# A recurrence that normalises its own input and output: two layer-norm stages folded into the LSTM loop of a hybrid convolution, attention and expert network

## The chip, the cores and the metric

The kernel runs on one core of a Trainium2 chip. A core has five engines that work side by side: PE (TensorE, matrix products), DVE (VectorE), ACT (ScalarE), POOL (GpSimd) and SP (SyncE, which here issues the DMAs). They wait for one another only through semaphores and through the barrier between two stages. The metric is the device time of one execution in microseconds (us). Before the change the median of three runs is 1300.95 us (1299.09 to 1301.1).

## The reference, cut to what matters

The network has many layers; this change touches the part between the slice attention and the sigmoid attention. The activations are 32 images of 64 channels by 256 positions, held on chip in `xa` as 128 partitions (two halves of the batch times 64 channels) by 4096 columns (16 images by 256 positions).

```
h = layernorm(x)                     # over the 64 channels, eps 1e-5        "ln3"
for t in range(256):                 # LSTM over the 256 positions, 32 sequences
    g = tanh(h_t U_c + s V_c + b_c);  i, o = sigmoid(h_t U_i + s V_i + b_i), sigmoid(... o ...)
    c = f * c + i * g                # the kernel keeps the cell in a scaled form
    s = o * tanh(c);  y_t = s
x = x + y                            # the residual
h = layernorm(x)                     # "ln4", the input of the sigmoid attention
```

A layer norm here is three steps: take the mean over 64 channels away (a product with the matrix `center`), sum the squares over the channels, and multiply with one over the root of the variance plus 1e-5.

## The kernel before, in words

The program is a row of stages. Each stage opens a block in which every engine has its own instruction list, and ends with a barrier of all engines; the next stage starts some 0.8 to 0.9 us later. Four stages matter here, in this order.

`slice_attention_stage` (line 1313) works through eight tiles of 512 columns in a software pipeline. Its SP list stores the row maxima of the recurrent weights to DRAM (`vrow`, line 1616) and loads them back to every partition (`vall`, line 1618). POOL has nothing to do in it.

`layer_norm_stage` with prefix "ln3" (line 1151) normalises all 4096 columns tile by tile: PE centres (line 1176), DVE copies the result out of PSUM (line 1234), ACT squares (line 1225), PE sums the squares (line 1183), ACT takes a root (line 1218), DVE inverts it (line 1251), PE spreads it over the channels (line 1196), and DVE multiplies (line 1257). For ln3 the result goes to `xn_steps`, ordered by time step, sixteen columns per step, so that DVE writes with a stride. During it DVE works out the scale of the recurrent weights (`recurrent_scale`), and POOL clears buffers and makes the two half-precision parts `vh` and `vl` of the weights (lines 1277 to 1301).

`lstm_stage` (line 1628) is the recurrence, 256 steps in a loop of 16 turns of 16 steps. One step:

- PE adds the product of the state with the three gate matrices to what already lies in PSUM: six products with `h1`, the half-precision state (line 1694), then three with `h2`, its remainder (line 1698). It waits for `h1_ready` and `h2_ready`.
- ACT takes the tanh of two gates (line 1715), of the third (line 1718), and later of the cell (line 1721).
- DVE updates the cell by a scan (line 1749), makes `og` (1754), `h1` (1759), the full state (1760), `h2` (1762) and the next step's addend `hc` (1763).

The input's part of the gates, with the bias, is prepared eight steps ahead in five parts (`prepare`, lines 1674, 1676, 1679, 1682): one part is issued after the state products of each of the first five steps of every eight. Parts 0 and 3 are the biases, parts 1, 2 and 4 read `xn_steps`. POOL, once every eight steps, scales the eight finished states (line 1730) and adds them to `xa` (line 1734). In every turn DVE also takes a maximum of the expert weights (line 1766).

`layer_norm_stage` with prefix "ln4" normalises `xa` again, in the same manner as ln3. During it SP stores the maxima of the expert weights to DRAM (line 1307) and loads them back (line 1309), because `sigmoid_attention_stage` (line 1770), which follows, needs their scale.

The order of the work around the change is written out by hand: the code that follows each step of the loop (`if k == ...`) says after which step an engine does which piece of the other work. An engine does its list in order, so a wait in one of these pieces holds up the next step's work on that engine.

Of the kernel before, what the change touches and what calls it, by code (L numbers as in the profile page):

```python
# [27 lines left out]
C = 64  # L28
# [1122 lines left out]
def layer_norm_stage(nc, m, prefix, out_view):  # L1151
# [3 lines left out]
    with ExitStack() as c:  # L1155
        def sb(name, shape):
# [6 lines left out]
                                 "spread_done", "xn_ready", "top_step", "cleared", "scaled", "halves", "top_stored",  # L1163
                                 "top_landed")}
# [66 lines left out]
        def _(dve):  # L1231
# [4 lines left out]
            def recurrent_scale():  # L1236
                r = m.rscale
                dve.tensor_reduce(r[:, 0:1], m.vall[:], AXX, ALU.max).then_inc(s["top_step"], 1)
                dve.wait_ge(s["top_step"], 1)
                dve.tensor_scalar(r[:, 0:1], r[:, 0:1], 2.0 ** -20, None, ALU.max).then_inc(s["top_step"], 1)  # L1240
                dve.wait_ge(s["top_step"], 2)
                bits = r[:, 0:1].bitcast(mybir.dt.int32)
                dve.tensor_scalar(bits, bits, 0x7F800000, None, ALU.bitwise_and).then_inc(s["top_step"], 1)
                dve.wait_ge(s["top_step"], 3)
                dve.reciprocal(r[:, 1:2], r[:, 0:1]).then_inc(s["top_step"], 1)
                dve.tensor_scalar(r[:, 2:3], r[:, 0:1], 1.0 / (VSCALE * HSCALE), None, ALU.mult)\
                   .then_inc(s["top_step"], 1)

# [11 lines left out]
            if prefix == "ln3":  # L1260
                recurrent_scale()
            if prefix == "ln4":
                dve.tensor_reduce(m.etop[:], m.wtop[:], AXX, ALU.max).then_inc(s["top_step"], 1)
# [10 lines left out]
        if prefix == "ln3":  # L1274
            @block.gpsimd
            def _(pool):
                pool.memset(m.terms[:], 0.0).then_inc(s["cleared"], 1)
                pool.memset(m.cells[:], 0.0).then_inc(s["cleared"], 1)
                pool.memset(m.h_unscale[:], 1.0 / HSCALE).then_inc(s["cleared"], 1)
                pool.memset(m.h1[:], 0.0).then_inc(s["cleared"], 1)  # L1280
                pool.memset(m.h2[:], 0.0).then_inc(s["cleared"], 1)
                pool.memset(m.xn_steps[:, COLS:], 0.0).then_inc(s["cleared"], 1)
                pool.wait_ge(s["cleared"], 1)
                pool.memset(m.factors.rearrange("p (b k) -> p b k", k=3)[:, :, 1], 1.0).then_inc(s["cleared"], 1)
                pool.memset(m.addends.rearrange("p (b k) -> p b k", k=3)[:, :, 0], 1.0).then_inc(s["cleared"], 1)
                pool.wait_ge(s["top_step"], 5)
                for g, n in enumerate("gio"):
                    half = 1.0 if n == "g" else 0.5
                    pool.tensor_scalar(m.vs[:, g, :], p[f"v_{n}"], m.rscale[:, 1:2], half * VSCALE, ALU.mult, ALU.mult)\
                        .then_inc(s["scaled"], 1)  # L1290
                    pool.tensor_scalar(m.u[:, g, :], p[f"u_{n}"], m.rscale[:, 1:2], half * VSCALE * HSCALE,
                                       ALU.mult, ALU.mult).then_inc(s["halves"], 1)
                pool.tensor_scalar(m.ls_bias[0:3, :], p["lstm_b"][0:3, :], p["lstm_half"][0:3, :], VSCALE * HSCALE,
                                   ALU.mult, ALU.mult).then_inc(s["halves"], 1)
                pool.wait_ge(s["halves"], 4)
                pool.tensor_scalar(m.ls_bias[0:3, :], m.ls_bias[0:3, :], m.rscale[0:3, 1:2], None, ALU.mult)\
                    .then_inc(s["halves"], 1)
                pool.wait_ge(s["scaled"], 3)
                pool.tensor_copy(m.vh[:], m.vs[:]).then_inc(s["scaled"], 1)
                pool.wait_ge(s["scaled"], 4)  # L1300
                pool.tensor_tensor(m.vl[:], m.vs[:], m.vh[:], ALU.subtract).then_inc(s["scaled"], 1)

        if prefix == "ln4":
            @block.sync
            def _(sp):
                sp.wait_ge(s["top_step"], 1)
                sp.dma_start(m.vrow.rearrange("o p -> p o"), m.etop[:]).then_inc(s["top_stored"], 16)
                sp.wait_ge(s["top_stored"], 16)
                sp.dma_start(m.vall[:], m.vrow.broadcast_to([P, P])).then_inc(s["top_landed"], 16)
                sp.wait_ge(s["top_landed"], 16)  # L1310


def slice_attention_stage(nc, m):
# [9 lines left out]
    with ExitStack() as c:  # L1323
        def sb(name, shape, dt=F32):
# [15 lines left out]
                 "out_ready v_top v_stored v_landed").split()  # L1340
# [7 lines left out]
        def run(engine, step):  # L1348

            step(-2, 0, True, False, False, False)  # L1350
            step(-1, 1, True, True, False, False)
            step(0, 0, True, True, True, False)
            with engine.Fori(0, TILES // 2 - 2) as i:
# [148 lines left out]
        def _(dve):  # L1502
# [108 lines left out]
            run(dve, step)  # L1611
# [9 lines left out]
        @block.gpsimd  # L1621
        def _(pool):

            pool.sem_inc(s["lt_done"], 2)
            pool.sem_inc(s["gt_done"], 2)
            pool.sem_inc(s["o_done"], 2)

def lstm_stage(nc, m):
# [9 lines left out]
    CH = STEPS * HB  # L1638
    SC = HSCALE
    with ExitStack() as c:  # L1640
        def sb(name, shape, dt=F32):
# [3 lines left out]
        hs = sb("hs", [P, 2 * STEPS, HB])  # L1645
        hx = sb("hx", [P, 2, STEPS, HB])
        to, tc = sb("to", [P, HB]), sb("tc", [P, HB])
        og = sb("og", [P, HB])
        names = ("warm z_done zo_done o_ready gates_ready cell_ready tc_ready og_ready h1_ready h32_ready h2_ready "
                 "hc_ready scaled out_ready").split()  # L1650
        u, bias, vh, vl, h1, h2 = m.u, m.ls_bias, m.vh, m.vl, m.h1, m.h2
        terms, cells, unscale, factors, addends = m.terms, m.cells, m.h_unscale, m.factors, m.addends
# [6 lines left out]
        xa_bt = m.xa[:].rearrange("p (b t) -> p b t", b=HB)  # L1659

        @block.tensor
        def _(pe):
# [21 lines left out]
            for part in range(5):  # L1684
                prepare(0, 0, part)
            with pe.Fori(0, HW // (2 * STEPS)) as i:
                for b in range(2):
                    for q in range(STEPS):
                        t = 2 * STEPS * i + STEPS * b + q
                        pe.wait_ge(s["h1_ready"], t + 1)  # L1690
                        ig, o = o_of(b, q)
                        for v in (vh, vl):
                            for g in range(3):
                                pe.matmul(ig[:, g, :] if g < 2 else o, v[:, g, :], h1[:],  # L1694
                                          start=False, stop=False, skip_group_check=True)
                        pe.wait_ge(s["h2_ready"], t + 1)
# [783 lines left out]
```

## Time and profile before

| what | value |
|---|---|
| median of 3 runs | 1300.95 us |
| profiled execution | 1295.79 us, its span 1294.0 us |
| PE busy | 990.2 us (77%) |
| DVE busy | 843.1 us (65%) |
| ACT busy | 514.9 us (40%) |
| POOL busy | 279.6 us (22%) |
| ln3, first instruction to the last | 433.64 to 452.69 us |
| recurrence, first state `h1` to the last | 458.32 to 870.01 us |
| ln4, first instruction to the last | 872.28 to 891.13 us |
| mean granted clock of PE | 0.783 |

The span is cut by the trace's own clock; the profiled execution is 5.2 us faster than the median of the runs. The page's slices show PE's granted clock at 0.5 (1.2 GHz) through the whole recurrence, and mostly at 0.8 to 1.0 before and behind it. Busy time on an engine tells little in the recurrence, because each engine in turn waits for the other two.

### The profile page before, as it was taken

What the parts mean: (1) busy time and instruction counts of PE and PEld (TensorE: products, weight loads), DVE (VectorE), ACT (ScalarE), POOL (GpSimd) and SP (SyncE); (2) the same over time, 40 slices, a digit from 0 to 9 for tenths busy, and PEclk for the clock granted to TensorE, in tenths of its full rate; (3) what the DMA queues carried; (4) which work ended last, traced back from release to release, by engine and by line L of the source; (5) the groups of instructions that cost most, each with busy time, mean ns of one, the idle gap of its engine ahead of it and who ended that gap; (6) DMA issues with size and microseconds to landing.
All of it is one profiled execution on the core that took longest, in us unless ns stands there. A gap on an engine that the chain in (4) does not pass through costs nothing. (4 is left out here: it accounts for less than half of the span.)

```text
span 1294.0 us, 23970 instructions
## 1 busy us (share of the span) xinstructions
PE 990.2 (77%) x8107; PEld 545.6 (42%) x8107; DVE 843.1 (65%) x2435; ACT 514.9 (40%) x1332; POOL 279.6 (22%) x393
## 2 busy tenths in 40 slices
PE   6878777677999666666666666658964999999996
PEld 2466552253667344444444444433522333333332
DVE  7787647735566645555555555554366888888885
ACT  3544534353444333333333333334532454545542
POOL 4604102200000100000000000000000465555655
PEclk9889988878999955555555555558986999999998
DMA  7000002000000000000000000000004655646550
GB/s 238 1 2 1 1 2 82 0 1 1 3 1 1 1 2 0 0 0 0 0 0 0 0 0 0 0 0 3 0 1 98 147 126 119 137 113 134 123 123 9
DMA packets 11251, 47.52 MB, mean 37 GB/s; under 512 B 1840, under 2 KB 6320, under 8 KB 6704
## 3 DMA queue, kind: packets, MB, share of 16 engines
q1 hardware_dynamic: 11184, 46.62, 14.9%
q8 instruction: 42, 0.69, 0.2%
q14 instruction: 25, 0.20, 0.1%
HBM read 43.99 MB, written 2.62 MB: 36 GB/s over the span
## 5 line engine op out<-in xcount | busy, mean ns | idle before, releaser
L2169 ACT ACTIVATE ex_gated<-wide,unscale 128x1024 f32<-128x1024 f32 x128 | 142.2, 1114 | 139.4 <-PE wide L2135 139.3
L2185 DVE TENSOR_TENSOR ex_hid<-wide,ex_gated 128x1024 f32<-128x1024 f32 x128 | 155.8, 1222 | 39.2 <-ACT ex_gated L2169 27.9
L1694 PE MATMUL wide<-h,vh 128*128 128x16 f16 x768 | 63.3, 181 | 152.2 <-DVE h L1759 152.2
L2111 POOL TENSOR_TENSOR ex_acc<-ex_part,ex_acc 128x512 f32<-128x512 f32 x120 | 152.6, 1272 | 95.3 <-DVE ex_part L2201 81.3
L1749 DVE TENSOR_TENSOR_SCAN cells<-terms 128x48 f32<-128x48 f32 x256 | 75.3, 294 | 111.2 <-ACT terms L1715 108.9
L1715 ACT ACTIVATE terms<-wide 128x32 f32<-128x32 f32 x256 | 54.6, 213 | 211.0 <-PE wide L1698 211.0
L1694 PEld LDWEIGHTS wide<-h,vh 128*128 128x128 f16 x768 | 40.3, 108 | 221.1 <-DVE h L1759 221.1
L2147 PE MATMUL wide<-ex_hid,w 128*64 128x512 f32 x512 | 116.7, 598 | 0.0
L2135 PE MATMUL wide<-xh,wh 64*128 64x512 f16 x512 | 99.0, 383 | 5.1 <-PEq L83 3.7
L1730 POOL TENSOR_TENSOR ls_hx<-ls_hs,h_unscale 128x128 f32<-128x128 f32 x32 | 14.6, 455 | 395.3 <-DVE ls_hs L1760 395.3
L2135 PE MATMUL wide<-xh,wl 64*128 64x512 f16 x512 | 98.3, 380 | 0.0
L2135 PE MATMUL wide<-xl,wh 64*128 64x512 f16 x512 | 98.2, 380 | 0.0
L2201 DVE SCALAR_TENSOR_TENSOR ex_part<-wide,unscale,ex_d 128x1024 f32<-128x1024 f32 x64 | 81.9, 1282 | 15.4 <-PE wide L2147 10.6
L1721 ACT ACTIVATE ls_tc<-cells 128x16 f32<-128x16 f32 x256 | 57.0, 223 | 77.3 <-DVE cells L1749 77.3
L1759 DVE TENSOR_TENSOR h<-ls_og,ls_tc 128x16 f16<-128x16 f32 x256 | 44.7, 175 | 57.1 <-ACT ls_tc L1721 57.1
L314 DVE SCALAR_TENSOR_TENSOR L_acc<-xpad,L_taps,L_acc 128x528 f32<-128x528 f32 x80 | 63.8, 867 | 3.7 <-ACT L_acc L257 3.6
L1698 PE MATMUL wide<-h,vh 128*128 128x16 f16 x768 | 63.8, 181 | 0.0
L2147 PEld LDWEIGHTS wide<-ex_hid,w 128*64 128x64 f32 x512 | 34.0, 136 | 68.6 <-issue 65.9
L215 PE MATMUL wide<-xpad,L_diag 128*128 128x512 f32 x96 | 47.8, 651 | 17.5 <-DVE L_diag L346 10.2
L1694 PE MATMUL wide<-h,vl 128*128 128x16 f16 x768 | 58.2, 174 | 0.0
L2135 PEld LDWEIGHTS wide<-xh,wh 64*128 64x128 f16 x512 | 25.1, 94 | 74.6 <-issue 29.4
L1763 DVE SCALAR_TENSOR_TENSOR terms<-ls_hs,cells 128x16 f32<-128x16 f32 x256 | 53.3, 208 | 0.0
(368 smaller groups left out, 1941.4 us busy)
## 6 DMA issues: line engine op xcount, KB each, us to landing
ex_d<-route SPq DMA_DIRECT2D x64, 512.0 KB, 6.5
par_attn<-in_attn SPq DMA_DIRECT2D x1, 2704.0 KB, 13.3
par_rest<-in_rest SPq DMA_DIRECT2D x1, 2523.5 KB, 18.7
L_xin<-in_x SPq DMA_DIRECT2D x8, 256.0 KB, 5.8
w<-in_w SPq DMA_DIRECT2D x1, 2048.0 KB, 8.2
out<-ex_acc SPq DMA_DIRECT2D x16, 128.0 KB, 3.3
w<-in_w SPq DMA_DIRECT2D x1, 512.0 KB, 9.1
route<-ro_dt SPq DMA_DIRECT2D x2, 256.0 KB, 2.0
```

Of the source, the lines that this page charges most:

```text
L314: dve.scalar_tensor_tensor(acc_rows(t), rows_of(t, q), taps[:, q:q + 1], acc_rows(t), ALU.mult, ALU.add).then_inc(tap_step, 1)
L1694: pe.matmul(ig[:, g, :] if g < 2 else o, v[:, g, :], h1[:], start=False, stop=False, skip_group_check=True)
L1698: mm = pe.matmul(ig[:, g, :] if g < 2 else o, vh[:, g, :], h2[:], start=False, stop=True, skip_group_check=True)
L1715: act.activation(two_gates, bank[b][:, 2 * q * HB:2 * (q + 1) * HB].rearrange("p (g b) -> p g b", g=2), ACT.Tanh, scale=back).then_inc(s[" ...
L1721: act.activation(tc[:], cell, ACT.Tanh, scale=0.5).then_inc(s["tc_ready"], 1)
L1749: dve.tensor_tensor_scan(cells[:].rearrange("p b k -> p (b k)"), factors, addends, 0.0, ALU.mult, ALU.add)\
L2111: pool.tensor_tensor(acc[:, t % 2, :], part[:, (e // 2) % 2, e % 2, :], acc[:, t % 2, :] if e else tile_of(m.xa, t), ALU.add)\
L2135: mm = pe.matmul(pair_of_up(G, j)[:, h * TW:(h + 1) * TW], weight[r, (2 * e + w) * HID:(2 * e + w + 1) * HID], x[r, t % 2, :], start=(n == ...
L2147: mm = pe.matmul(pair_of_down(G, r)[C * h:C * (h + 1), n % 2 * TW:(n % 2 + 1) * TW], m.w3[:, n % E * C:(n % E + 1) * C], hid[:, n % (2 * G ...
L2169: act.activation(gated[:, n % 2, :], pair_of_up(n // GS, 2 * (n % GS))[:], ACT.Silu, scale=m.unscale[:, 0:1]).then_inc(s["gated_ready"], 1)
L2185: dve.tensor_tensor(hid[:, n % (2 * GS), :], pair_of_up(n // GS, 2 * (n % GS) + 1)[:], gated[:, n % 2, :], ALU.mult).then_inc(s["hid_ready ...
L2201: dve.scalar_tensor_tensor(part[:, r], pair_of_down(G, r)[:].rearrange("p (e n) -> p e n", e=2), m.unscale[:, 0:1], d[:, G % GT, 2 * r:2 * ...
```

## The change

Both layer-norm stages around the recurrence are taken out, and the recurrence does their work, 256 columns (16 steps) at a time. In turn i it normalises the columns of turn i+1 (`_in`) and those that turn i-1 has finished (`_out`). The first and the last turn are written out ahead of and behind the loop. The roots of the two groups are taken together, by eleven small DVE instructions (an estimate from the bits, then three Newton steps), each of which waits for the one before it. DVE adds every state to `xa` itself, 16 columns per step with a stride of 256 columns; POOL has no list in this stage. DVE's `recurrent_scale` and POOL's preparation of the weights move into the slice attention stage. The store and load of the expert weights' maxima move from ln4 to the end of `lstm_stage`.

```diff
 slice_attention_stage:   run(dve, step)  ->  run(dve, step, recurrent_scale)   # after step 0
+        @block.gpsimd: memsets; wait top_step 5; vs, u, ls_bias; vh, vl        # as in ln3 before
-def lstm_stage(nc, m):
+def lstm_stage(nc, m, normed):
+    dev(n) = bank[4 + 2 * n][:, 0:2 * P];  spread(n) = bank[4 + 2 * n][:, 2 * P:4 * P]
+    sums(n) = bank[5][:, 4 * n:4 * n + 4];  stream(j) = xa_bt[:, :, 16 * j : 16 * j + 16]
         @block.tensor
+            def centre_in(j):
+                pe.matmul(dev(0), p["center"], stream(j).rearrange("p b t -> p t b"), ...)   # in_centred
+            def sums_in(j):
+                pe.wait_ge(s["in_squared"], j + 1)
+                for k in range(2):
+                    mm = pe.matmul(sums(0)[:, 2 * k:2 * k + 2], sq[:, 0, k * P:(k + 1) * P], by_half, ...)
+            def turn_in(j):
+                pe.wait_ge(s["in_spread"], j + 1)
+                for k in range(2):
+                    mm = pe.transpose(spread(0)[:, k * P:(k + 1) * P], wide_root[:, 0, ...], p["ident"])
+            # centre_out, sums_out, turn_out: the same with n = 1; centre_out reads stream(j) as it lies
             def body(i, first, last):            # behind the nine state products of step k
+                    if k == 0 and not last:  centre_in(i + 1)
+                    if k == 1 and not first: centre_out(i - 1)
+                    if k == 2 and not last:  sums_in(i + 1)
+                    if k == 3 and not first: sums_out(i - 1)
+                    if k == 4:               prepare(2 * i + 1, 1, 0)
+                    if k == 5:               prepare(..., 1);  prepare(..., 2)
+                    if k == 6:               prepare(..., 3);  prepare(..., 4)
+                    if k == 8 and not last:  prepare(2 * i + 2, 0, 0)
+                    if k == 9 and not last:  prepare(2 * i + 2, 0, 3)
+                    if k == 10:              turn_in(i + 1);  turn_out(i - 1)
+                    if k == 12 and not last:
+                        pe.wait_ge(s["in_ready"], i + 2)
+                        prepare(2 * i + 2, 0, 1);  prepare(2 * i + 2, 0, 2)
+                    if k == 13 and not last: prepare(2 * i + 2, 0, 4)
         @block.scalar                            # behind the tanh of the cell of step k
+                    if k == 0: square_in(i + 1)          # waits in_centred;  128x256 from PSUM
+                    if k == 1: move_in(i + 1);  square_out(i - 1)
+                    if k == 2: move_out(i - 1)
+                    if k == 9: spread_in(i + 1);  spread_out(i - 1)
+            def spread_in(j):
+                act.wait_ge(s["root_step"], 11 * (j + 1))
+                act.activation(wide_root[:, 0, :] as 4 x 64, root[:, 1, IN] broadcast to 64, ACT.Copy)
-        @block.gpsimd                            # hx = hs * unscale;  xa = hx + xa, once in 8 steps
         @block.vector
+            def root_step(n, k, of):
+                if k:  dve.wait_ge(s["root_step"], 11 * n + k)
+                # k = 0: v = sums + 1e-5; 1: y from the bits; then a = -v/2*y, a = a*y, y = (a+1.5)*y
+            def scale_in(j):                     # waits in_turned, in_moved
+                dve.tensor_tensor(xn_steps[:, 256 columns], spread(0), moved[:, 0, :], ALU.mult)
             def body(i, first, last):            # behind hc of step k
+                    x = xa_bt[:, :, bass.ds(t, 1)]
+                    dve.scalar_tensor_tensor(x, h32[:], 1.0 / SC, x, ALU.mult, ALU.add)   # every step
+                    if 4 <= k < 9:  root_step(i + 1, 2 * (k - 4), of);  root_step(i + 1, 2 * (k - 4) + 1, of)
+                    if k == 9:      root_step(i + 1, 10, of)
+                    if k == 11 and not last:  scale_in(i + 1)
+                    if k == 12 and not first: scale_out(i - 1)
+                    if k == 14: tensor_reduce of the expert weights   # was behind step 11
+                if last:  dve.tensor_reduce(m.etop[:], m.wtop[:], AXX, ALU.max)
+        ahead of the loop: ACT loads the register `back`; centre_in(0), square_in(0), move_in(0), sums_in(0),
+            eleven root steps, spread_in(0), turn_in(0), scale_in(0), then prepare(0, 0, 1), (0, 0, 2), (0, 0, 4)
+        behind it: centre_out(15), square_out(15), sums_out(15), ACT.Sqrt, DVE reciprocal, spread, turn_out(15),
+            scale_out(15)
+        @block.sync
+            sp.wait_ge(s["top_found"], TURNS + 1)
+            sp.dma_start(m.vrow, m.etop[:]);  sp.wait_ge(s["top_stored"], 16)
+            sp.dma_start(m.vall[:], m.vrow.broadcast_to([P, P]));  sp.wait_ge(s["top_landed"], 16)
 build:
-            layer_norm_stage(nc, m, "ln3", normed_by_step)
-            lstm_stage(nc, m)
-        layer_norm_stage(nc, m, "ln4", normed)
+            lstm_stage(nc, m, m.xn.rearrange("p (b t) -> p b t", b=HB))
```

The diff above is shortened: helper definitions are put on one line, and the buffers and semaphores are left out.

## Rows read from the trace of the kernel before

**Rows 1.** Timeline of one step; columns: start, duration, instruction, idle before
```profile
459.90 0.17 DVE L1759 TENSOR_TENSOR h<-ls_og,ls_tc 128x16 f16<-128x16 f32 x1 [0.22 <-ACT ls_tc L1721]
...
460.13 0.25 PE L1694 MATMUL wide<-h,vh 128*128 128x16 f16 x3 [0.36 <-DVE h L1759]
...
460.29 0.18 DVE L1763 SCALAR_TENSOR_TENSOR terms<-ls_hs,cells 128x16 f32<-128x16 f32 x1
...
460.43 0.25 PE L1698 MATMUL wide<-h,vh 128*128 128x16 f16 x3
...
460.68 0.21 ACT L1715 ACTIVATE terms<-wide 128x32 f32<-128x32 f32 x1 [0.81 <-PE wide L1698]
...
460.93 0.26 DVE L1749 TENSOR_TENSOR_SCAN cells<-terms 128x48 f32<-128x48 f32 x1 [0.47 <-ACT terms L1715]
...
461.22 0.22 ACT L1721 ACTIVATE ls_tc<-cells 128x16 f32<-128x16 f32 x1 [0.27 <-DVE cells L1749]
...
461.48 0.18 DVE L1759 TENSOR_TENSOR h<-ls_og,ls_tc 128x16 f16<-128x16 f32 x1 [0.22 <-ACT ls_tc L1721]
```
**Rows 2.** Windows: us, busy (instructions) of PE, PEld, DVE, ACT, POOL; granted clock
```profile
455.00:460.00 5.00, 4.77 (x30) 3.27 (x29) 1.28 (x10) 0.99 (x6) 0.00 (x0) 0.50 0.00 0
```
**Rows 3.** Timeline, DVE in the eighth step, while POOL runs
```profile
469.75 0.45 DVE L1763 SCALAR_TENSOR_TENSOR terms<-ls_hs,cells 128x16 f32<-128x16 f32 x1
...
470.39 0.58 DVE L1749 TENSOR_TENSOR_SCAN cells<-terms 128x48 f32<-128x48 f32 x1 [0.20 <-ACT terms L1715]
```
**Rows 4.** Timeline from the start of ln3 to the first state of the recurrence
```profile
433.65 1.28 ACT L1213 ACT_TABLE_LOAD   x1 [7.58 <-PEq L83]
...
434.00 0.15 DVE L1240 TENSOR_SCALAR rscale<-rscale 128x1 f32<-128x1 f32 x1
...
434.19 0.15 DVE L1243 TENSOR_SCALAR rscale<-rscale 128x1 int32<-128x1 int32 x1
...
454.62 1.22 PE L1676 MATMUL wide<-xn_steps,u 128*128 128x128 f32 x4
...
456.50 0.80 PE L1682 MATMUL wide<-xn_steps,u 128*128 128x128 f32 x2
...
457.08 0.27 PE L1694 MATMUL wide<-h,vh 128*128 128x16 f16 x3
...
458.32 0.18 DVE L1759 TENSOR_TENSOR h<-ls_og,ls_tc 128x16 f16<-128x16 f32 x1 [0.23 <-ACT ls_tc L1721]
```
**Rows 5.** Waits by total, 345 to 425 us: waiter, releaser, us, times, longest
```profile
DVE sl_gtm L1585 <- PE wide L1437: 12.1, 6, 2.1
```
**Rows 6.** Timeline from the last state to the sigmoid attention; then line 1309's landing
```profile
870.01 0.18 DVE L1759 TENSOR_TENSOR h<-ls_og,ls_tc 128x16 f16<-128x16 f32 x1 [0.22 <-ACT ls_tc L1721]
...
872.52 0.32 SPq L1307 DMA_DIRECT2D vrow<-etop  x1
...
879.74 0.32 SPq L1309 DMA_DIRECT2D vall<-vrow  x1
...
892.04 1.28 ACT L1864 ACT_TABLE_LOAD   x1 [5.67 <-PEq L83]
...
DMA to landing us min/median/max: 4.7/4.7/4.7
```
**Rows 7.** Groups by line and shape: xcount, busy us, mean ns, idle before
```profile
L1721 ACT ACTIVATE ls_tc<-cells 128x16 f32<-128x16 f32 x256 | 57.0, 223 | 77.3 <-DVE cells L1749 77.3
...
L1225 ACT ACTIVATE ln_sq<-ln_dev 128x512 f32<-128x512 f32 x32 | 20.0, 629 | 15.4 <-DVE ln_dev L1234 15.4
...
L848 DVE TENSOR_TENSOR att_ysum<-wide,att_den 128x256 f32<-128x256 f32 x20 | 7.5, 418 | 0.4
...
L1257 DVE TENSOR_TENSOR xn_steps<-wide,ln_dev 128x512 f32<-128x512 f32 x8 | 7.1, 1006 | 0.2 <-PE wide L1196 0.2
...
L600 PE MATMUL wide<-att_val,par_attn 128*128 128x128 f32 x64 | 7.7, 277 | 0.0
...
L1766 DVE TENSOR_REDUCE wtop<-w x16 | 6.6, 411 | 0.0
```

More of the change, by code:

```diff
@@ L1346, in slice_attention_stage, with run @@
         XP, XT, TM, LG, ET, GT, OB = bank[0], bank[1], bank[2], bank[3:5], bank[5], bank[6], bank[7]
-        def run(engine, step):
+        def run(engine, step, between=None):
             step(-2, 0, True, False, False, False)
@@ L1352, in run @@
             step(0, 0, True, True, True, False)
+            if between:
+                between()
             with engine.Fori(0, TILES // 2 - 2) as i:
@@ new lines, in _ @@
+            centre_in(0)
+            prepare(0, 0, 0)
+            prepare(0, 0, 3)
+            sums_in(0)
+            turn_in(0)
+            pe.wait_ge(s["in_ready"], 1)
+            for part in (1, 2, 4):
+                prepare(0, 0, part)
+            body(0, True, False)
+            with pe.Fori(1, TURNS - 1) as i:
+                body(i, False, False)
+            body(TURNS - 1, False, True)
+            centre_out(TURNS - 1)
+            sums_out(TURNS - 1)
+            turn_out(TURNS - 1)
@@ new lines, in move_out, with spread_out, body @@
+            def move_out(j):
+                act.activation(moved[:, 1, :], dev(1), ACT.Copy).then_inc(s["on_moved"], 1)
+            def spread_out(j):
+                act.wait_ge(s["root_step"], 11 * (j + 3))
+                act.activation(wide_root[:, 1, :].rearrange("p (n c) -> p n c", n=4),
+                               root[:, 1, OUT].unsqueeze(2).broadcast_to([P, 4, C]), ACT.Copy)\
+                   .then_inc(s["on_spread"], 1)
+            def body(i, first, last):
+                for k in range(2 * STEPS):
+                    b, q = k // STEPS, k % STEPS
+                    t = 2 * STEPS * i + k
+                    act.wait_ge(s["z_done"], t + 1)
+                    act.activation(two_gates, bank[b][:, 2 * q * HB:2 * (q + 1) * HB].rearrange(
+                        "p (g b) -> p g b", g=2), ACT.Tanh, scale=back).then_inc(s["gates_ready"], 1)
+                    act.wait_ge(s["zo_done"], t + 1)
+                    act.activation(to[:], bank[2 + b][:, q * HB:(q + 1) * HB], ACT.Tanh, scale=back)\
+                       .then_inc(s["o_ready"], 1)
+                    act.wait_ge(s["cell_ready"], t + 1)
+                    act.activation(tc[:], cell, ACT.Tanh, scale=0.5).then_inc(s["tc_ready"], 1)
+                    if k == 0 and not last:
+                        square_in(i + 1)
+                    if k == 1 and not last:
+                        move_in(i + 1)
+                    if k == 1 and not first:
+                        square_out(i - 1)
+                    if k == 2 and not first:
+                        move_out(i - 1)
+                    if k == 9 and not last:
+                        spread_in(i + 1)
+                    if k == 9 and not first:
+                        spread_out(i - 1)
@@ new lines, in _ @@
+            square_in(0)
+            move_in(0)
+            act.activation(tc[:, 0:1], p["ident"][:, 0:1], ACT.Tanh).then_inc(s["warm"], 1)
+            spread_in(0)
+            body(0, True, False)
+            with act.Fori(1, TURNS - 1) as i:
+                body(i, False, False)
+            body(TURNS - 1, False, True)
+            act.activation(root[:, 0, 0:1], p["ident"][:, 0:1], ACT.Sqrt).then_inc(s["warm"], 1)
+            square_out(TURNS - 1)
+            act.wait_ge(s["on_summed"], TURNS)
```

371 lines of the change are left out of this document (233 added, 138 removed).

## The prediction

> **What bounds the kernel now.** I read the page's slices first (no engine is full from 452 to 872 us), then the timeline of one step, then the borders of the stages. They show a circle rather than a full engine: in the brackets behind the instructions ACT waits 0.81 us for PE's state products, DVE 0.47 for ACT, PE 0.36 for DVE [rows 1]. The circle is the step. Call H the start of DVE's `h1` (459.90). PE starts on it at H+0.23, the products with `h2` start at H+0.53, ACT's gates at H+0.78, the scan at H+1.03, the tanh of the cell at H+1.32, the next `h1` at H+1.58 [rows 1]. So the recurrence is 255 intervals of 1.58 us plus whatever holds an engine up. Its span from first to last `h1` is 870.01 - 458.32 = 411.69 us [rows 4, 6]; 255 x 1.58 is 402.9, so 8.8 us is extra. The idle room inside a step is the other thing to see: DVE ends `hc` at H+0.57 (0.39 + 0.18, and such an instruction lets the next one start 0.10 after it, at H+0.49) and has until H+1.03; ACT ends the cell's tanh at H+1.54 and has until the next gates at H+2.36; PE can take other work from about H+0.60 to H+1.81. Work that fits there is free, and work that is late is paid in full, because every step waits for it.
>
> **The change part by part.** Sums are made on the profiled execution (1295.79 us) and its differences taken from the median of the runs, 1300.95.
>
> *Entry.* From the start of ln3 (433.65) to the first `h1` (458.32) there are 24.67 us [rows 4]. In its place: the register load on ACT, which the trace doesn't show (0 to 2.5 us, since it hides between ACT's first tanh of the stage and the first gates; I take 1.0); square 0.4; eight half-size passes of the sums 0.75; eleven root steps at the spacing of dependent DVE instructions, 434.19 - 434.00 = 0.19, so 2.1 [rows 4]; spread 0.42; two transposes 0.5 (by 0.277 each [rows 7]); scaling 0.42 by the 128x256 row of 418 ns [rows 7]; semaphores between these, 0.4. That is 6.0. Then three prepare parts that need the result. Today four passes of 128 columns, a bias part and two more passes take 457.08 - 454.62 = 2.46 to the state products, and the bias part about 0.75 of it: 1.7 is left; from there to the first `h1` 458.32 - 457.08 = 1.24 [rows 4]. Together 8.9: **15.8 saved** (14 to 17).
>
> *POOL leaves.* When POOL runs, once in eight steps, DVE's `hc` takes 0.45 instead of 0.18 and the scan 0.58 instead of 0.26 [rows 1, 3]. 31 such places at 0.27 to 0.32, 8.4 to 9.9 us, and the 8.8 above agree: **9 saved**. DVE's own addition takes its place at H+0.49, ends about H+0.67, and the scan isn't due before H+1.03. Its stride costs little: the strided write of 512 columns takes 1006 ns in all [rows 7], so 16 columns can hardly pay more than 0.03. Cost 0.
>
> *Spreading the roots, behind step 9.* The last root step follows the addition, H+0.59, and ends at about H+0.76, so ACT starts `spread_in` at H+0.80, two hundredths after it could have started the next gates. ACT does its list in order, so the gates of step 10 wait for both spreads. One of 128x256 is between 128x16, 223 ns, and 128x512, 629 ns [rows 7]: 0.42, and neighbours on ACT overlap by up to 0.1, so two hold the gates until H+1.42 to H+1.64. Delay 0.64 to 0.86; I take 0.7. Fourteen middle turns at 0.7, the two outer ones at 0.35: **10.5 lost**. This is the cover that isn't there: all other ACT pieces stand where ACT waits 0.8 us anyway.
> The Trainium skill (ScalarE: Activation LUTs, What ACT_TABLE_LOAD costs) gives an ACTIVATE without pointer operands 186 ns and 0.833 ns per column, and an overlap of 93 ns; by that the pair would take 0.61, the delay 0.63, and this term 9.5 instead of 10.5.
>
> *The wait for `in_ready`, behind step 12.* DVE scales in step 11, H+0.59 to H+1.01, just before its scan. PE starts parts 1 and 2 at H+1.07 instead of H+0.60. Two passes let the state products start 457.08 - 456.50 = 0.58 later, and four take 1.22 - 0.80 = 0.42 more [rows 4]: 1.0, so H+2.07 against H+1.81. Of these 0.26 the products with `h2`, which come 0.30 later anyway, swallow 0.08. Fifteen turns at 0.18: **2.7 lost** (0 to 6).
>
> *What just fits.* Behind step 0 the two passes of 256 columns of `centre_in` are as many columns as four passes of 128, 1.22 [rows 4]: H+0.60 to H+1.82. ACT squares from H+1.86 to H+2.26, before the gates at H+2.36. Behind step 1 `move_in` and `square_out` end at H+2.35: level. Behind steps 2 and 3 four weight loads with two columns each take less than those four passes. Steps 5 and 6 carry two parts: 1.0 and 1.3, against 1.2 of room. On DVE the root steps come in pairs at 0.19: H+0.59, H+0.78, done at H+0.95 before H+1.03; the reduction of 411 ns [rows 7] behind step 14 ends at H+1.0. Seven of these have under 0.1 to spare; together I give them 0.1 per turn: **1.6 lost** (0 to 15).
>
> *Slice stage.* `recurrent_scale` puts five dependent instructions, 1.05 us, into DVE's list after step 0. Six times in that stage DVE waits for PE, up to 2.1 us each, behind these places [rows 5]; POOL's work beside it stretches a few DVE instructions. **0.3 lost** (0 to 1).
>
> *Exit.* Before, the sigmoid attention starts 892.04 - 870.01 = 22.03 after the last `h1`. Call that `h1` T. The chain of the last 256 columns now is: addition T+0.67, centring 1.2, square 0.4, sums 1.0, root 0.3, reciprocal and spread 0.6, transposes 0.6, scaling 0.42, so about T+5.7. But it isn't last. The store of the maxima takes 879.74 - 872.52 = 7.22 and the load back 4.7 [rows 6]; ln4 hid both. Now the last maximum is made behind step 255's addition, SP issues at T+0.8, and the load lands at T+12.7; with the border of 0.9 the next stage starts at T+13.6. **8.4 saved**, and 7 us of what the diff seems to promise here goes to the DMA.
>
> *Sum.* -15.8 - 9 + 10.5 + 2.7 + 1.6 + 0.3 - 8.4 = **-18.1**. The profiled execution would be 1277.7, the median 1282.8.
>
> **The rivals.**
> *A. The strided read.* `centre_in` reads one column in 256 of `xa` (step order), which no product before does. Runs of four columns are free: 277 ns per pass [rows 7] like the packed ones. If a single column then costs what a run of four does, 256 columns take four times as long as at the full clock, twice as long as at 1.2 GHz, 0.85 us more: fifteen times 0.85 is 12.8 lost, 1295.6. Chance 0.12.
> The Trainium skill (SBUF — State Buffer, Door 1: The DMA port swizzle) speaks for it: SBUF is read in lines of 16 bytes, and each access that crosses to a new line pays. By that rule alone it would be this rival's time.
> *B. Slower.* The same place decides: the reader is PE, the next step's `h1` is due at H+1.81, and the saving is used up when the read takes 18.1/15 = 1.2 us more than a packed one. Against it: DVE's strided columns take 1006/512 = 1.96 ns each in all [rows 7], and a packed column already has (1.22 - 0.80)/256 = 1.64 ns in the loop [rows 4]; for it only that no PE row exists. At three times a packed read (+1.7 us) the time is 1282.8 + 25.5 = 1308. Chance 0.08.
> *C. DVE has no room.* If the root pairs, the two scalings and the reduction (eight steps per turn) each push the scan by 0.15, 19 us go and the time is 1301. For it: margins under 0.1. Against it: the reduction of 411 ns [rows 7] stands in the same gap today, and the 8.8 us are all POOL's. Chance 0.07.
> *D. The clock rises in the loop.* It falls to 0.5 before the recurrence, and PE that was busy 4.77 of 5 us at its start was still at 0.5, the lower level [rows 2]. The new loop keeps PE busier. If it rose in part, the path from `h2` to the gates would shorten by some 0.05 to 0.1 on half the steps and the late parts would shrink: 10 more saved, 1273. Chance 0.10.
> *E. The normalisation doesn't stay in the loop's gaps on ACT:* the waits for the centred columns push the gates behind steps 0 and 1 by 0.2 each, 6 lost, 1289. Chance 0.08.
>
> **How the numbers follow.** The forecast as summed has 0.55. The range takes the entry, the wait and the small pushes at their ends, from 1300.95 - 29 to 1300.95 - 4 (A included): 1272 to 1297. Faster by over 0.2% (2.6 us, about what a measurement of this kernel can tell) holds the forecast, A, D and E: 0.85. Within 0.2%: half of C, 0.04. Slower: B and the other half, 0.11.
>
> **What would show it.** Right: no interval of 1.88 between states; fifteen intervals of about 2.3 behind step 9, ending in ACT's gates with two spreads ahead of them; 1.76 behind step 12; all others 1.58 to 1.63; first `h1` about 9 us after the slice stage's border; the last DMA landing 12.7 us after the last `h1`, with all engines idle for 7. Wrong: an interval of 2.4 behind step 0 (A, B), intervals of 1.7 at steps 4 to 8 (C), a granted clock of 1.0 in the loop (D), or a stage that ends with its last multiplication.

## The result, and the profile after

The changed kernel takes **1280.7 us** (median of 4 runs, 1279.49 to 1281.23) where the kernel before takes 1300.02 (4 runs on the same chip, 1298.93 to 1301.1): a ratio of **0.985**, 95% interval 0.9833 to 0.9867. The forecast was 1282.8 in 1272 to 1297.

The kernel before scatters more than the changed one: over the two later comparisons its executions lay between 1293.8 and 1301.8, with medians of 1295.82 (12 runs) and 1299.28 (9 runs). Its profiled execution (1295.79, span 1294.0) is a short one, that of the changed kernel (1281.04, span 1279.2) is not. So the medians differ by 19.3 and the spans by 14.8, and everything below that is counted in parts is counted between the spans. The parts, from starts in the two timelines:

```
part                                                        before    after   difference
start of the span to the slice stage's addend of tile 0     317.72   318.82      +1.1
from there to the last operation of the slice stage         114.31   114.32       0.0
last operation of the slice stage to the first h1            26.29    11.73     -14.6
first h1 to the last h1 (255 intervals)                     411.69   417.49      +5.8
last h1 to the first instruction of the sigmoid attention    22.03    14.26      -7.8
from there to the end                                       401.96   402.58      +0.6
```

The first part is code that didn't change; it drifts between executions (the slice stage ended between 430.32 and 434.13 in the profiles of eight kernels with the changed kernel's code up to there). Hence a median settles an edit of 8 us here but not one of 1 us, and the parts do.

The page of the changed kernel, its first part and PE's granted clock in 40 slices:
```profile
PE 1021.4 (80%) x8065; PEld 585.7 (46%) x8065; DVE 860.2 (67%) x2877; ACT 530.9 (41%) x1404; POOL 248.7 (19%) x327
...
PEclk9988988878899855555555555556986999999998
```
Busy time hardly tells anything: PE is up by 31 us and the kernel is faster. What the change brings lies at the borders of the stage, -14.6 and -7.8; in the loop it takes POOL's 9 us away and adds more than that.

**The entry**, in the timeline of the changed kernel; it answers to [rows 4] (columns as there):
```profile
434.82 1.08 PE L1689 MATMUL wide<-xa,par_rest 128*128 128x256 f32 x2 [1.72 <-PEq L83]
...
435.94 0.38 ACT L1795 ACTIVATE ls_sq<-wide 128x256 f32<-128x256 f32 x1 [8.77 <-PE wide L1689]
...
437.21 1.01 PE L1695 MATMUL wide<-par_rest,ls_sq 128*128 128x2 f32 x4
...
438.34 0.16 DVE L1866 TENSOR_SCALAR ls_root<-wide 128x4 f32<-128x4 f32 x1 [4.45 <-PE wide L1695]
...
440.51 0.41 ACT L1802 ACTIVATE ls_wide_root<-ls_root 128x256 f32<-128x256 f32 x1 [3.82 <-DVE ls_root L1875]
...
442.18 1.23 PE L1680 MATMUL wide<-xn_steps,u 128*128 128x128 f32 x4 [0.52 <-DVE xn_steps L1881]
...
444.87 0.18 DVE L1906 TENSOR_TENSOR h<-ls_og,ls_tc 128x16 f16<-128x16 f32 x1 [0.23 <-ACT ls_tc L1830]
```
Centring, square, sums, eleven root steps, spread, transposes, scaling, three prepare parts, in a row. The square is done at 436.32 and the sums start at 437.21: two bias parts stand between them in PE's list.

**The loop.** Differences between the starts of successive `h1`, one line per turn, in us (worked out from the timeline):
```
behind step        0    1    2    3    4    5    6    7    8    9   10   11   12   13   14   15
first turn       1.57 1.58 1.58 1.59 1.57 1.58 1.68 1.60 1.58 1.86 1.58 1.58 1.72 1.58 1.58 1.58
a loop turn      1.58 1.58 1.58 1.58 1.57 1.58 1.68 1.58 1.58 2.16 1.59 1.58 1.87 1.57 1.58 1.59
last turn        1.58 1.58 1.58 1.58 1.58 1.58 1.67 1.58 1.58 1.85 1.58 1.59 1.58 1.57 1.59
before, a turn   1.57 1.58 1.58 1.58 1.58 1.57 1.58 1.88 1.58 1.58 1.57 1.58 1.58 1.58 1.58 1.87
```
The two of 1.88 per turn are gone, three other places are late. The largest is behind step 9, in the timeline of the changed kernel:
```profile
537.52 0.17 DVE L1906 TENSOR_TENSOR h<-ls_og,ls_tc 128x16 f16<-128x16 f32 x1 [0.22 <-ACT ls_tc L1830]
...
538.09 0.16 DVE L1875 SCALAR_TENSOR_TENSOR ls_root<-ls_root 128x8 f32<-128x8 f32 x1
...
538.28 0.41 ACT L1802 ACTIVATE ls_wide_root<-ls_root 128x256 f32<-128x256 f32 x1 [0.80 <-DVE ls_root L1875]
538.61 0.40 ACT L1815 ACTIVATE ls_wide_root<-ls_root 128x256 f32<-128x256 f32 x1
...
538.91 0.19 ACT L1824 ACTIVATE terms<-wide 128x32 f32<-128x32 f32 x1
...
539.14 0.26 DVE L1897 TENSOR_TENSOR_SCAN cells<-terms 128x48 f32<-128x48 f32 x1 [0.89 <-ACT terms L1824]
...
539.68 0.17 DVE L1906 TENSOR_TENSOR h<-ls_og,ls_tc 128x16 f16<-128x16 f32 x1 [0.22 <-ACT ls_tc L1830]
```
Read the bracket of the first spread: ACT waited 0.80 us, until H+0.76, for a root, and then put two spreads ahead of gates that wait for nothing. DVE's scan, next in the circle, pays.

**The exit**, in the timeline of the changed kernel; it answers to [rows 6]:
```profile
862.36 0.18 DVE L1906 TENSOR_TENSOR h<-ls_og,ls_tc 128x16 f16<-128x16 f32 x1 [0.22 <-ACT ls_tc L1830]
...
862.93 0.16 DVE L1933 TENSOR_REDUCE etop<-wtop 128x1 f32<-128x16 f32 x1
...
863.12 0.32 SPq L1960 DMA_DIRECT2D vrow<-etop  x1
...
867.39 0.42 DVE L1887 TENSOR_TENSOR xpad<-wide,ls_moved 128x256 f32<-128x256 f32 x1 [0.78 <-PE wide L1722]
870.28 0.32 SPq L1962 DMA_DIRECT2D vall<-vrow  x1
876.62 1.28 ACT L2060 ACT_TABLE_LOAD   x1 [10.54 <-PEq L83]
```
The last multiplication ends at 867.81, the next stage's first instruction is at 876.62. Between them there is a DMA issue and nothing else. For 7.7 of these 8.8 us the core waits for 128 numbers to come back (they land 5.2 us after the issue, at about 875.5); the rest is the border between two stages.

### The profile page after: what moved, and what is told of

Its sections match the earlier page's. It is cut to its first block and busy times, and to the rows that moved or that the text cites. A ratio compares the mean times of both kernels' runs of the same rounds, so it can differ in the third digit from the quotient of the medians.

```text
span 1279.2 us, 24547 instructions
## 1 busy us (share of the span) xinstructions
PE 1021.4 (80%) x8065; PEld 585.7 (46%) x8065; DVE 860.2 (67%) x2877; ACT 530.9 (41%) x1404; POOL 248.7 (19%) x327
## 5 line engine op out<-in xcount | busy, mean ns | idle before, releaser
L1733 PEld LDWEIGHTS wide<-h,vh 128*128 128x128 f16 x768 | 46.0, 112 | 161.5 <-DVE h L1906 159.5
L1897 DVE TENSOR_TENSOR_SCAN cells<-terms 128x48 f32<-128x48 f32 x256 | 66.0, 258 | 71.6 <-ACT terms L1824 64.8
L2005 POOL COPY sg_x<-xpad 128x512 f32 x8 | 4.8, 613 | 558.9 <-SPq L1970 524.0
L1909 DVE TENSOR_TENSOR h<-ls_h,h 128x16 f16<-128x16 f32 x256 | 44.7, 175 | 8.8
```

The source lines that it names most:

```text
L1733: pe.matmul(ig[:, g, :] if g < 2 else o, v[:, g, :], h1[:], start=False, stop=False, skip_group_check=True)
L1897: dve.tensor_tensor_scan(cells[:].rearrange("p b k -> p (b k)"), factors, addends, 0.0, ALU.mult, ALU.add)\
```

## The experiments

All eight that follow are counted by the same parts as above, each from one profile: the entry (last operation of the slice stage to the first `h1`), the loop (first to last `h1`) and the exit (last `h1` to the sigmoid attention). The changed kernel has entry 11.73, loop 417.49, exit 14.26. Ratios are to the kernel before: the first four share 12 runs of it, the next three 9. The sixth and the eighth kernel ran once, so they rest on the parts alone.

**1. Spread a step later.** The spreads move from ACT's list behind step 9 to behind step 10, the transposes from 10 to 11.
```diff
-                    if k == 9 and not last:   spread_in(i + 1)      # and spread_out
+                    if k == 10 and not last:  spread_in(i + 1)
-                    if k == 10 and not last:  turn_in(i + 1)        # and turn_out
+                    if k == 11 and not last:  turn_in(i + 1)
```


> The changed kernel with both spreads of the roots on ACT behind step 10 instead of 9, and the transposes on PE behind step 11 instead of 10. Theory (ACT's spreads hold the gates of step 10, because the last root step ends just when those gates could start): the intervals of 2.16 behind step 9 go back to 1.58, 14 x 0.58 + 2 x 0.28 = 8.7 us less than the changed kernel, about 1272.0. Rival (the long interval comes from DVE's root steps or from the transposes, or merely moves to step 10): under 2 us less, a long interval again behind step 9 or 10.

Measured: 1271.36 us (1269.65 to 1273.77, 5 runs), ratio to before 0.98 (0.977 to 0.983). The loop is 408.61, 8.88 shorter; every interval behind step 9 is 1.58 and the others are as they were. The timeline of this kernel at that place:
```profile
536.59 0.22 ACT L1830 ACTIVATE ls_tc<-cells 128x16 f32<-128x16 f32 x1 [0.27 <-DVE cells L1897]
536.72 0.40 ACT L1802 ACTIVATE ls_wide_root<-ls_root 128x256 f32<-128x256 f32 x1
536.84 0.17 DVE L1906 TENSOR_TENSOR h<-ls_og,ls_tc 128x16 f16<-128x16 f32 x1 [0.22 <-ACT ls_tc L1830]
...
537.02 0.40 ACT L1815 ACTIVATE ls_wide_root<-ls_root 128x256 f32<-128x256 f32 x1
...
537.63 0.21 ACT L1824 ACTIVATE terms<-wide 128x32 f32<-128x32 f32 x1 [0.21 <-PE wide L1737]
```
The same two instructions of the same length, without a wait in front, end 0.21 us before the gates are due. So the 8.9 us were the wait for the root, not the work.

**2. Prepare a step later.** Parts 1 and 2 move behind step 13, part 4 behind step 14.
```diff
-                    if k == 12 and not last:   # wait in_ready; prepare parts 1, 2
+                    if k == 13 and not last:
-                    if k == 13 and not last:   # prepare part 4
+                    if k == 14 and not last:
```


> The changed kernel with parts 1 and 2 of the preparation, and their wait for in_ready, behind step 13 instead of 12, part 4 behind step 14. Theory (PE waits for DVE's scaling and starts the two parts 0.5 late): the intervals of 1.87 behind step 12 become 1.58, 14 x 0.29 + 0.14 = 4.2 us less than the changed kernel, about 1276.5. Rival (two parts with four passes are too long for the gap wherever they stand): no change, the 1.87 moves to step 13.

Measured: 1273.97 us (1270.24 to 1277.07, 6 runs), ratio 0.9821 (0.9792 to 0.985). The loop is 413.06, 4.43 shorter: all intervals of 1.87 are 1.58, but for one of 1.72 in the first turn of the loop. Its other intervals are unchanged.

**3. Maxima sent early.** The last maximum of the expert weights is taken in the first turn, the one over all of them behind step 0 of the last turn, so the two DMAs run beside the last 15 steps.
```diff
-                    if k == 14:                # maximum of the turn's weights
+                    if k == 14 and not last:
-                if last:                       # etop, behind step 15
+                    if k == 13 and first:      # the maximum of turn 15
+                    if k == 0 and last:        # etop
```


> The changed kernel with the last maximum of the expert weights taken in the first turn and their joint maximum behind the first step of the last turn, so that the store and the load back start 24 us earlier. Theory (the exit is held by these two DMAs, 12 us in a row): the stage ends with its last multiplication, 5.5 us after the last state instead of 13.4, 7.9 us less than the changed kernel, about 1272.8. Rival (the DMAs land late but the barrier or the last normalisation would hold the border anyway): under 2 us less.

Measured: 1272.3 us (1271.84 to 1273.1, 5 runs), ratio 0.9807 (0.9779 to 0.9836). Exit 6.51, 7.75 shorter; loop 417.38. The timeline of this kernel, from the two DMAs to the next stage:
```profile
838.08 0.32 SPq L1964 DMA_DIRECT2D vrow<-etop  x1
845.11 0.32 SPq L1966 DMA_DIRECT2D vall<-vrow  x1
...
861.38 0.17 DVE L1906 TENSOR_TENSOR h<-ls_og,ls_tc 128x16 f16<-128x16 f32 x1 [0.22 <-ACT ls_tc L1830]
...
866.42 0.42 DVE L1887 TENSOR_TENSOR xpad<-wide,ls_moved 128x256 f32<-128x256 f32 x1 [0.78 <-PE wide L1722]
867.89 1.28 ACT L2064 ACT_TABLE_LOAD   x1 [2.79 <-PEq L83]
```
Now the stage ends with its multiplication (866.84), and the next begins 1.05 after it.

**4. One part alone: the kernel before, with DVE's addition.** POOL's list is taken out of the recurrence, DVE adds 16 columns per step.
```diff
-                    pool.tensor_tensor(hx, hs, unscale, ALU.mult);  pool.tensor_tensor(x, hx, x, ALU.add)
+                        x = xa_bt[:, :, bass.ds(t, 1)]
+                        dve.scalar_tensor_tensor(x, h32, 1.0 / SC, x, ALU.mult, ALU.add)
```


> The kernel before, with only POOL's two operations per eight steps replaced by DVE's addition in every step. Theory (POOL slows DVE's hc and scan once in eight steps, and DVE's own addition is hidden): all intervals 1.58, 9.2 us less than before, about 1290.8. Rival (DVE's addition with its stride delays every scan by 0.05 or more): 13 us more and 9 less, no faster than before.

Measured: 1289.33 us (1288.28 to 1291.38, 7 runs), ratio 0.9937 (0.9914 to 0.996). The loop is 402.68 against 411.69: 9.0 shorter, and all 255 intervals are 1.57 to 1.59. DVE's addition is free, and POOL's work was the only thing that held the old loop up. The whole kernel gained less, 6.9 between the spans and 6.5 between the medians: of the 9.0, 0.5 went to the exit (22.48), 1.1 to the part behind it (403.11) and 0.5 to the first part, and the last two are code that didn't change. Against this loop the whole change costs 14.8 us in its loop (417.49), and saves 22.4 at its two ends. One step of this kernel, to lay beside [rows 3]:
```profile
469.90 0.17 DVE L1749 TENSOR_TENSOR h<-ls_og,ls_tc 128x16 f16<-128x16 f32 x1 [0.22 <-ACT ls_tc L1721]
...
470.29 0.17 DVE L1753 SCALAR_TENSOR_TENSOR terms<-ls_hs,cells 128x16 f32<-128x16 f32 x1
470.38 0.18 DVE L1756 SCALAR_TENSOR_TENSOR xa<-ls_hs,xa 128x16 f32 x1
470.93 0.26 DVE L1739 TENSOR_TENSOR_SCAN cells<-terms 128x48 f32<-128x48 f32 x1 [0.37 <-ACT terms L1715]
```

**5. Half of the change.** Only the next 256 columns are normalised in the loop; ln4 stays a stage behind it and carries the DMAs, as before.
```diff
-    centre_out, sums_out, turn_out, square_out, move_out, spread_out, scale_out and the code behind the loop
+        layer_norm_stage(nc, m, "ln4", normed)      # its SP list stores and loads the maxima
```


> The changed kernel with only the input's normalisation in the loop; the output is normalised by the separate stage ln4 as before, with the two DMAs of the maxima in it. Theory: one spread instead of two costs 0.28 instead of 0.58 behind step 9, the loop is 412.5 instead of 417.5 us, the exit 22.0 again instead of 14.3; 2.8 us more than the changed kernel, so the output's half of the change is worth only about 3 us as it stands. Rival (the output's half costs nothing in the loop, being hidden): the loop stays at 417, 7.7 us more than the changed kernel.

Measured: 1282.91 us (1279.25 to 1284.82, 5 runs), ratio 0.987 (0.9846 to 0.9893). Loop 412.60, exit 21.63. Against the whole change the loop is 4.9 shorter, and nearly all of that is the second spread (1.86 instead of 2.16, fourteen times, and 1.58 instead of 1.86 in the last turn); the exit is 7.4 longer. So the finished columns' norm was worth 2.5 us as it was built.

**6. Sums first.** At the entry the sums go ahead of the two bias parts.
```diff
             centre_in(0)
+            sums_in(0)
             prepare(0, 0, 0)
             prepare(0, 0, 3)
-            sums_in(0)
```


> The changed kernel with sums_in(0) ahead of the two bias parts on PE before the first turn. Theory (PE does its list in order and the bias parts kept the sums waiting from 436.3 to 437.2): the first state comes 0.9 us earlier after the slice stage, 10.8 instead of 11.7 us. Rival (the chain of eleven root steps and the register load set the entry): no change.

Measured: 1278.24 us (1 run). Entry 10.90, 0.83 shorter, loop 417.22, exit 14.44.

**7. All of them together,** and part 4 moved from behind step 6 to behind step 7: experiments 1, 2, 3 and 6, and
```diff
                     if k == 6:
                         prepare(2 * i + 1, 1, 3)
+                    if k == 7:
                         prepare(2 * i + 1, 1, 4)
```


> The changed kernel with five moves: the spreads behind step 10 and the transposes behind 11; parts 1 and 2 behind step 13 and part 4 behind 14; of the two parts behind step 6 one behind 7; the expert weights' maxima 24 us earlier; at the entry the sums of squares ahead of the two bias parts. Theory (the loop loses only to these three late pieces, the exit only to the DMAs): all 255 intervals 1.58, the loop 402.6 us instead of 417.5, exit 6.5 instead of 14.3, entry 0.9 shorter; 23.6 us less than the changed kernel, about 1257. Rival (the gaps are full, so that a piece moved away pushes the step it goes to): the loop stays above 408, about 1263 or more.

Measured: **1257.63 us** (1257.43 to 1260.36, 5 runs), ratio to the kernel before **0.9687** (0.9667 to 0.9708). Entry 10.90, loop 403.53, exit 6.51. The 1.68 behind step 6 is 1.58. What is left lies behind step 12: one interval of 1.87 in the first turn of the loop, and 1.64 in each of the thirteen turns after it, 1.0 us together. In the first of them DVE stands still for 0.34 us before its scaling of the finished columns, and the trace names no releaser, only the issue:
```profile
487.04 0.18 DVE L1914 SCALAR_TENSOR_TENSOR xa<-ls_h,xa 128x16 f32 x1
...
487.56 0.43 DVE L1888 TENSOR_TENSOR xpad<-wide,ls_moved 128x256 f32 x1 [0.34 <-issue]
...
487.91 0.25 DVE L1898 TENSOR_TENSOR_SCAN cells<-terms 128x48 f32<-128x48 f32 x1
```
The long one happens once. In the other turns the scaling starts 0.28 after the addition (in the changed kernel 0.17, 543.32 to 543.49), ends later, and DVE's next scan starts 0.08 late:
```profile
512.61 0.18 DVE L1914 SCALAR_TENSOR_TENSOR xa<-ls_h,xa 128x16 f32 x1
512.89 0.42 DVE L1888 TENSOR_TENSOR xpad<-wide,ls_moved 128x256 f32 x1
...
513.24 0.25 DVE L1898 TENSOR_TENSOR_SCAN cells<-terms 128x48 f32<-128x48 f32 x1
```
Why the scaling starts late was not settled. In the kernel of experiment 2 the same place stands at 1.58. The granted clock stays at 0.50 from 445 to 845 us here too, with PE busy for 313.6 of 400 us.

**8. The strided read by itself.** `centre_in` reads 256 neighbouring columns of a weight in place of the input's columns that lie 256 apart. The recurrence then works on the wrong input, so only its times are of use.
```diff
-                pe.matmul(dev(0), p["center"], stream(j).rearrange("p b t -> p t b"), ...)
+                pe.matmul(dev(0), p["center"], p["w_x"], ...)
```


> The changed kernel, but centre_in reads 256 neighbouring columns of a weight tensor (w_x) instead of the 256 columns of xa that lie 256 columns apart, so the recurrence gets another input: that part of the computation is replaced. Everything else stands. In the changed kernel the two products of centre_in take 1.08 us at the entry, where the granted clock is 1.0, and 1.20 us in the loop, at 0.5. Theory (a single strided column costs PE about 2 ns to read, whatever the clock, which at 1.2 GHz hides behind the 1.6 ns that every column takes there anyway, and at 2.4 GHz doesn't): the entry's two products take 0.60 to 0.70 us (the packed 512-column products take 1.12 for two at the full clock, 0.56 for half the columns), so the entry is 0.4 shorter, 11.3; in the loop the pair still takes 1.2 and behind step 0 the interval stays at 1.58, so the loop is 417.2 to 417.6 as in the changed kernel. Rival 1 (the 1.08 is the clock, which had not fully risen, or fixed cost): 1.08 again, entry 11.7. Rival 2 (rival A of the prediction in the loop too): the pair in the loop falls to 0.8 and some of the loop's small pushes go, 1 to 3 us.

Measured: 1279.67 us (1 run). The entry in the timeline of this kernel:
```profile
434.72 0.67 PE L1689 MATMUL wide<-par_rest 128*128 128x256 f32 x2 [1.72 <-PEq L83]
435.32 0.70 PE L1678 MATMUL wide<-par_rest,ls_bias 3*128 3x256 f32 x2
435.87 0.52 PE L1683 MATMUL wide<-par_rest,ls_bias 3*128 3x128 f32 x2
436.32 1.01 PE L1695 MATMUL wide<-par_rest,ls_sq 128*128 128x2 f32 x4
...
443.02 1.20 PE L1689 MATMUL wide<-par_rest 128*128 128x256 f32 x2
```
The pair takes 0.67 instead of 1.08 at the entry, and 1.20 in the loop, where with the stride it takes 1.20 to 1.22. The tensor that is read changed with the stride, and only one distance was run. The loop is 417.48. The entry is 10.93, twice the expected gain: the granted clock falls from 1.0 to 0.5 at about 436 in both kernels, and what is 0.4 earlier, the first bias part, still runs before the fall (0.70 instead of 1.02; PE's next two products, 0.52 instead of 0.63, are a little shorter too). The windows of this kernel and of the changed one show the fall (columns as in [rows 2]):
```profile
435.50:436.00 0.50, 0.50 (x4) 0.42 (x3) 0.00 (x0) 0.50 (x3) 0.00 (x0) 0.97 0.00 0
436.00:436.50 0.50, 0.50 (x4) 0.28 (x3) 0.00 (x0) 0.17 (x2) 0.00 (x0) 0.50 0.00 0
```
```profile
435.50:436.00 0.50, 0.50 (x2) 0.17 (x2) 0.00 (x0) 0.06 (x1) 0.00 (x0) 1.00 0.00 0
436.00:436.50 0.50, 0.50 (x2) 0.40 (x3) 0.00 (x0) 0.50 (x3) 0.00 (x0) 0.58 0.00 0
```

## Why the prediction was right, step by step

The profiled execution was to be 1277.7 and is 1281.04. Of the 3.3 us between them 1.2 are the entry, 0.6 the exit, and 1.7 lie in the first and the last part of the table, which no step of the prediction covered; 0.3 for the slice stage, which weren't lost, go the other way. The loop came out at +5.8 as summed, but partly by errors that cancel. That the median, 1280.7, is nearer to its forecast of 1282.8 than the profiled execution is to its own is luck: the medians differ by 19.3 and the spans by 14.8, because the kernel before scatters and its profile was a short one.

*POOL leaves* (-9): right, -9.0 with that edit alone (experiment 4). The addition at no cost: right as well.

*Spreading the roots, behind step 9* (+10.5): the mechanism is right (experiment 1), the size was 8.8: fourteen intervals are longer by 0.58 to 0.59 (0.7 was taken, of 0.64 to 0.86) and the outer two by 0.28. The root was done at H+0.73 and the spreads started 0.33 and 0.30 apart, less than the row's length suggested. By the 186 ns, 0.833 ns per column and 93 ns of overlap that the Trainium skill gives (ScalarE: Activation LUTs, What ACT_TABLE_LOAD costs) one takes 0.40 and the next starts 0.31 later; the trace agrees, with 0.41 and 0.30 to 0.33, and the 9.5 worked out from it was the nearer one.

*The wait for `in_ready`, behind step 12* (+2.7): right place (experiment 2), too small, 4.2: 0.29 in fourteen turns and 0.14 in the first. The first turn gives the reason, since its code is the same with fixed addresses. The scaling and the first pass of the parts in the first turn, then in a turn of the loop:
```profile
463.12 0.18 DVE L1913 SCALAR_TENSOR_TENSOR xa<-ls_h,xa 128x16 f32<-128x16 f32 x1
463.21 0.42 DVE L1881 TENSOR_TENSOR xn_steps<-wide,ls_moved 128x256 f32<-128x256 f32 x1
...
463.69 1.22 PE L1680 MATMUL wide<-xn_steps,u 128*128 128x128 f32 x4 [0.27 <-DVE xn_steps L1881]
...
541.74 0.18 DVE L1913 SCALAR_TENSOR_TENSOR xa<-ls_h,xa 128x16 f32 x1
541.89 0.43 DVE L1881 TENSOR_TENSOR xn_steps<-wide,ls_moved 128x256 f32 x1
...
542.47 1.22 PE L1680 MATMUL wide<-xn_steps,u 128*128 x4 [0.43 <-DVE xn_steps L1881]
```
With fixed addresses the scaling starts 0.09 after the addition and PE 0.06 after its end; with addresses from the loop's register it is 0.15 and 0.15. That is the 0.15 by which 0.29 exceeds 0.14. The prediction took the distances of fixed addresses. In the fourteen turns with addresses from the register, and only there, the trace has a register instruction on DVE's list in front of the scaling, of 0.06 to 0.07 us, apparently for the address (columns: count, duration in ns as shortest/median/longest, first and last start in us):
```profile
L1881 DVE TENSOR_TENSOR xn_steps<-wide,ls_moved x16: 419/425/426, 441.7 to 830.7; 128x256 f32 x14, 128x256 f32<-128x256 f32 x2
L1881 DVEq FUSED_REGOPS  x14: 64/71/71, 489.2 to 830.6; - x14
```
That the register's address is what costs is read from these rows; no run changed it alone.

*What just fits* (+1.6): 1.5, but not spread over seven places: sixteen times 0.09 to 0.10 behind step 6, where two parts run (gone in experiment 7), and nothing anywhere else. Rival C, which had every gap on DVE overflow, is false: its places stand at 1.58, except behind steps 6, 9 and 12, and those go back when pieces of PE and ACT are moved and DVE's stay (experiments 7, 1 and 2). Only in the kernel of experiment 7 does DVE itself push its scan, behind step 12. (By its own figures rival C adds up to 1302, not 1301.)

*Slice stage* (+0.3): 0.0.

*Entry* (-15.8): -14.6. From the stage's first instruction to the first `h1` it is 10.05 and not 8.9. The register load, taken at 1.0, hid behind PE's and DVE's work; the centring, 1.1, was missing from the list, and the two cancel. What failed is the sums: 0.75 was given to them, for eight passes, as if nothing stood ahead. They are four products of two columns each; they start 0.89 late behind the bias parts and take 1.01 at the lower clock. Experiment 6 takes 0.83 of it back.

*Exit* (-8.4): -7.8. SP issues at T+0.76 (T+0.8), the multiplication ends at T+5.45 (T+5.7), the load lands at about T+13.1 (T+12.7, since it took 5.2 and not 4.7) and the next stage starts at T+14.26 (T+13.6), 1.1 behind the landing instead of 0.9. Experiment 3 shows that the DMA's round trip was the whole remainder.

*Rivals A and B* asked whether a strided column costs PE more. In the loop it costs nothing that counts: 1.20 to 1.22 us per pair against 1.20, and no late interval behind step 0. At the full clock it does, 1.08 against 0.67, 0.41 for 512 columns in all. The rule cited for rival A (SBUF — State Buffer, Door 1: The DMA port swizzle, in the Trainium skill) agrees in direction with what the trace shows at the higher clock, 1.6 times the packed time and not the four times that rival A took; at 1.2 GHz the product itself needs the time anyway. That the lines of 16 bytes are the reason is not shown. *Rival D*: the clock was 0.50 from the first step to the last. *Rival E*: the intervals behind steps 0 and 1 are 1.58.

*The range.* It doesn't follow from the terms that it names: with the entry, the wait and the small pushes at their ends the sum runs from -23.6 to +0.4, not from -29 to -4. The measured -19.3 lies in both.

What the prediction priced but didn't question is the hand-written order: two moves by one step, one part moved, the sums placed first and the DMAs sent early give back 8.9 + 4.4 + 1.5 + 0.8 + 7.8 = 23.4 us by the single experiments (the 1.5 from the intervals of experiment 7). All together the entry, the loop and the exit are 22.5 us shorter, as 1.0 comes back behind step 12. That is more than the change itself brings. (The spans differ by 23.5; the last 1.0 of it lies in code that didn't change.)

## What to carry to other kernels

In a loop whose steps form a circle over several engines, place foreign work behind the instruction whose input it needs by a full step: a piece that would fit costs nearly its whole length once it starts with a wait in front of work that is ready. Find such places in the list of intervals between one marker instruction, which names the step, and then in the bracket of the first instruction that isn't the circle's. When a stage is folded away, ask what it hid, above all a DMA round trip, and start that where its input can be had, not where the stage ended.

## What the hardware showed that was not expected

- A product that reads single columns 256 apart takes 1.08 us per 2 x 256 columns at the granted clock 1.0 against 0.67 for neighbouring ones (of another tensor), and 1.20 to 1.22 against 1.20 at 0.5.
- Time saved ahead of a fall of the clock can count twice: in both kernels the clock fell 2.9 us after the last operation of the slice stage, and 0.41 us saved on the centring made the entry 0.80 shorter, in one profile of each.
- An instruction whose address comes from the loop's register starts 0.06 (DVE) to 0.09 us (PE, after a wait) later than the same one with a fixed address.
- POOL's scaling and addition stretch DVE's small instructions from 0.18 to 0.45 and from 0.26 to 0.58 us; without them the 255 intervals vary by 0.02.
- In the sigmoid attention the granted clock rises from 0.5 to 1.0 some 6.6 us after the stage's first instruction instead of 3.7 (worked out from windows of both kernels), so that the first eight score products take 2.08 us instead of 1.13. The 10.15 us for which PE stands idle ahead of the stage (4.34 before, behind ln4) don't explain it: in the kernel of experiment 2 PE is idle for 10.65 us and these products take 1.13, in that of experiment 7 it is idle for 2.40 and they take 1.87. When the clock rises differs from execution to execution here, and what sets it stays open. It is one part of the +0.6 in the table's last line.
